# Attention results divided two heads per position at a time, and ScalarE zeroing the first key blocks

## The reference

```
x = x + tanh(g_xattn[0]) * retention(ln(x), ctx)                  # 2 heads of 128, group norm, gate
x = x + tanh(g_ffn[0])   * mixture_of_experts(ln(x))              # 8 experts, the first of the top 2
x = x + tanh(g_xattn[1]) * grouped_attention(ln(x), ctx)          # 32 query heads, 8 key/value groups, head size 8
x = x + tanh(g_ffn[1])   * sparse_ffn(ln(x))                      # 256 -> 1024, 2:4 sparsified, -> 256

# grouped_attention, as far as the change touches it
attn = softmax(masked_scores)                     # causal, per head
out  = einsum('bnghm,bmgd->bnghd', attn, v)       # here: unnormalized sums, and a ninth column with the sum of weights
return out.reshape(B, S, D) @ w_o.T + b_o
```

## Time and profile before

| | us |
|---|---|
| median of 3 runs | 356.65 (356.33 to 358.82) |
| the profiled execution | 355.62 |
| its span | 353.5 |
| TensorE busy in the span | 316.3 (89%) |
| VectorE busy | 265.9 (75%) |
| ScalarE busy | 167.6 (47%) |
| GpSimd busy | 109.6 (31%) |

### The profile page before, as it was taken

The page is one execution under the profiler, slowest core; times in us unless marked ns, Lnnn a source line. Parts: engine busy times, 40 slices in busy tenths (PEclk is TensorE's granted clock), DMA queues, the critical chain, the costliest instruction groups (busy, mean ns, idle before and its releaser), DMA issues.

```text
span 353.5 us, 5149 instructions
## 1 busy us (share of the span) xinstructions
PE 316.3 (89%) x1671; PEld 218.0 (62%) x1671; DVE 265.9 (75%) x582; ACT 167.6 (47%) x341; POOL 109.6 (31%) x156
## 2 busy tenths in 40 slices
PE   2899886669999988999989999998979999899997
PEld 1495675647899634554644564463443787688896
DVE  4348896675677749989967996897585559999992
ACT  2433464344444223136767765775685434333320
POOL 7502675172000275601333424433555101000000
PEclk9999999559999999999999999999999999999999
DMA  6999300025321213700000000000000000000001
GB/s 231 359 413 295 67 1 16 2 89 174 106 67 59 77 59 111 307 0 9 0 7 2 0 1 9 0 3 0 7 2 1 0 2 0 2 0 1 30 32 59
DMA packets 14090, 22.96 MB, mean 65 GB/s; under 512 B 2065, under 2 KB 11409, under 8 KB 13202
## 3 DMA queue, kind: packets, MB, share of 16 engines
q1 hardware_dynamic: 13298, 20.56, 17.2%
q0 software_dynamic: 768, 2.10, 1.8%
HBM read 16.36 MB, written 6.03 MB: 63 GB/s over the span
## 4 chain that ended last, share of the span: by engine, by line
PE 57%; DVE 20%; issue 7%; POOL 6%; DMA 5%; ACT 4%; SPq 1%; DVEq 0%; ACTq 0%; POOLq 0%
PE bank L276 40%; DVE mx L1351 7%; PE bank L496 5%; PE bank L464 4%; ACT region L1024 3%; DVE stats L1097 3%; PE bank L467 2%; POOL x_sorted L821 2%; PE bank L292 2%; POOL rstd L789 2%; DVE x_sb L1137 1%; PE bank L511 1%; PE bank L286 1%; DMA x_sb<-in_x_dram 1%; DVE kblk L1270 1%
## 5 line engine op out<-in xcount | busy, mean ns | idle before, releaser
L1024 ACT ACTIVATE region<-bank,padcol 128x512 f32<-128x512 f32 x96 | 62.3, 692 | 18.7 <-PE bank L276 17.9
L1351 DVE TENSOR_REDUCE mx<-bank 128x2 f32<-128x512 f32 (+1 forms) x96 | 60.9, 683 | 4.8 <-PE bank L467 4.4
L857 POOL TENSOR_SCALAR_AFFINE_SELECT region<-region 128x1024 f32<-128x1024 f32 x32 | 35.8, 1121 | 77.9 <-ACT region L1024 77.8
L276 PE MATMUL bank<-qst,kblk 128*128 128x512 f32 x96 | 45.7, 487 | 0.8 <-DMA qst<-nmT 0.3
L464 PE MATMUL bank<-kblk,qst 128*128 128x512 f32 x96 | 43.6, 470 | 1.6 <-DVE mx L1351 1.2
L467 PE MATMUL bank<-causb,identb 128*128 128x256 bf16 (+1 forms) x96 | 30.6, 319 | 0.0
L789 POOL TENSOR_TENSOR rstd<-veps,power 128x1 f32<-128x1 f32 x40 | 25.7, 643 | 3.3
L785 POOL TENSOR_SCALAR veps<-mv 128x1 f32<-128x1 f32 x40 | 12.8, 320 | 40.7 <-DVE mv L1099 40.6
L276 PEld LDWEIGHTS bank<-qst,kblk 128*128 128x128 f32 x96 | 18.5, 197 | 9.2 <-ACT region L1024 6.6
L496 PE MATMUL bank<-region,vaug 128*32 128x512 f32 x192 | 23.9, 600 | 0.2
L464 PEld LDWEIGHTS bank<-kblk,qst 128*128 128x128 f32 x96 | 18.3, 190 | 8.8 <-issue 4.1
(11 more groups left out here) (205 smaller groups left out, 783.7 us busy)
## 6 DMA issues: line engine op xcount, KB each, us to landing
e_gu<-in_e_gu_dram SPq DMA_DIRECT2D x2, 1408.0 KB, 12.3
x_sorted<-zero SPq DMA_DIRECT2D x1, 1920.0 KB, 9.6
y_sorted<-region SPq DMA_DIRECT2D x15, 128.0 KB, 1.7
x_sb<-in_x_dram SPq DMA_DIRECT2D x4, 256.0 KB, 4.0
ctxT<-in_ctxT_dram SPq DMA_DIRECT2D x2, 512.0 KB, 6.4
e_down<-in_e_down_dram SPq DMA_DIRECT2D x1, 1024.0 KB, 14.0
region<-x_sorted SPq DMA_DIRECT2D x1, 1024.0 KB, 7.6
e_gu<-in_f_gate_dram SPq DMA_DIRECT2D x1, 1024.0 KB, 6.2
```

The lines of the kernel that those rows point to most:

```text
L276: return pe.matmul(dst, lhsT, rhs, start=first, stop=last)
L857: pool.affine_select(out=block, in_=block, compare_op=ALU.is_ge, fill=0.0, base=0, pattern=[[0, 2], [0, PER_GROUP], [1, P]], channel_multi ...
L1024: taken(act.activation(dst, src.rearrange("p (h n) -> p h n", n=SEQ - mt * P), ACT.Exp, bias=padcol[:, key:key + 1], scale=float(HD) ** -0 ...
L1351: taken(dve.reduce_max(mx[:, b % 2, nt, quads, q, hg], src, AX), "sa")
```

## The change

Two things. The division in `finish` is done for two head positions at a time: c = 0 and c = 2 now each make four transposes into the whole of bank 6, one reciprocal of 128x16 and one product of 128x128; c = 1 and c = 3 do nothing. Counts of semaphores follow. And `kblk[0]` is zeroed by ScalarE, with two copies of 128x1024 from the tile of zeros, behind the last copy to `xT` and ahead of the routing's exponential; GpSimd's two memsets and its wait for them are gone. `kblk[1]` is still zeroed by GpSimd.

```
+HEAD_PAIRS = (0, 2)
-        rden = sb("rden", [P, 2, HALVES, QUADS])
+        rden = sb("rden", [P, 2, 2, GROUPS])
 # TensorE, finish
-                if c < PER_GROUP:
-                    f = 4 * i + c
+                if c in HEAD_PAIRS:
+                    f = 2 * i + c // 2
                     dst = acquire(pe, "avT", f, "turn1")
 ...
-                    for q in range(HALVES):
-                        ins = pe.transpose(dst[:, tile_cols(q)], avT[nt][:, q, c * P:(c + 1) * P], ident[:, :])
+                    for h in range(2):
+                        for q in range(HALVES):
+                            ins = pe.transpose(dst[:, tile_cols(HALVES * h + q)], avT[nt][:, q, tile_cols(c + h)], ident[:, :])
                     ready(ins, "avT")
                 elif c == PER_GROUP:
-                    pe.wait_ge(sem("avT_taken"), 4 * i + 4)
+                    pe.wait_ge(sem("avT_taken"), 2 * i + 2)
                     turn_pair("atT", i, att[:, i % 2, :], "turn1")
-                else:
+                elif c > PER_GROUP:
 # GpSimd
-            pool.wait_ge(sem("res0_ready"), TILES)
-            pool.wait_ge(sem("rs_taken"), RET_HEADS)
-            clear_blocks(0)
-            pool.wait_ge(sem("blocks_clear"), HALVES)
-
 # ScalarE
+            act.wait_ge(sem("constants_set"), 1)
+            act.wait_ge(sem("res0_ready"), TILES)
+            act.wait_ge(sem("rs_taken"), RET_HEADS)
+            for q in range(HALVES):
+                act.activation(kblk[0][q], zero[:, :].unsqueeze(1).to_broadcast([P, QUADS, SEQ]), ACT.Copy)\
+                   .then_inc(sem("blocks_clear"), 1)
+
             act.wait_ge(sem("routed"), 2)
             act.activation(r_s[:, 3, :], r_s[:, 2, :], ACT.Exp).then_inc(sem("tanh_vexp"), 1)
 ...
-                        act.wait_ge(sem("avT_ready"), 8 * (b - 1) + 4 * nt + 4)
+                        act.wait_ge(sem("avT_ready"), 4 * (b - 1) + 2 * nt + 2)
 # VectorE, finish (value_copy has the same new count)
-                if c < PER_GROUP:
-                    o = att[:, i % 2, :].rearrange("p (q j h d) -> p h q j d", q=HALVES, j=QUADS, h=PER_GROUP)
-                    f = 4 * i + c
-                    src = filled(dve, "avT", f)[:, 0:2 * P].rearrange("p (q j r) -> p q j r", q=HALVES, j=QUADS)
+                if c in HEAD_PAIRS:
+                    o = att[:, i % 2, :].rearrange("p (g h d) -> p h g d", g=GROUPS, h=PER_GROUP)
+                    f = 2 * i + c // 2
+                    src = filled(dve, "avT", f).rearrange("p (h g r) -> p h g r", h=2, g=GROUPS)
                     dve.reciprocal(rden[:, f % 2, :, :], src[:, :, :, HD]).then_inc(sem("rden_made"), 1)
                     dve.wait_ge(sem("rden_made"), f + 1)
-                    taken(dve.tensor_tensor(out=o[:, c, :, :, :], in0=src[:, :, :, 0:HD],
-                                            in1=rden[:, f % 2, :, :].unsqueeze(3).to_broadcast([P, HALVES, QUADS, HD]),
+                    taken(dve.tensor_tensor(out=o[:, c:c + 2, :, :], in0=src[:, :, :, 0:HD],
+                                            in1=rden[:, f % 2, :, :].unsqueeze(3).to_broadcast([P, 2, GROUPS, HD]),
                                             op=ALU.mult), "avT")
```

More of the change, by code:

```diff
@@ L1388, in value_copy @@
                 if b >= 1:
-                    dve.wait_ge(sem("avT_ready"), 8 * (b - 1) + 4 * nt + 4)
+                    dve.wait_ge(sem("avT_ready"), 4 * (b - 1) + 2 * nt + 2)
                 taken(dve.tensor_copy(avT[nt][:, 0, :], src), "av0")
```

## The result

| | before | after |
|---|---|---|
| median, same chip | 356.49 us (355.0 to 358.82, 4 runs) | 352.08 us (350.91 to 352.6, 4 runs) |
| ratio | | 0.9887, interval 0.9856 to 0.9919 |
| profiled execution | 355.62 | 352.60 |
| its span | 353.5 | 350.8 |

The change makes the kernel 1.1% faster, 4.41 us by the medians, against 4.82 predicted. By the interval the gain of the runs lies between 2.9 and 5.1 us. The lines of the program have moved: L1197 is now L1201, L1402 is L1406, L1404 is L1408, L511 is L513 and L276 is L277.

What follows compares the result with a forecast made beforehand. It took routing's cross-engine chain, and VectorE pacing TensorE in passes 1 and 2, as the bounds. Clear 1.52 plus pairs 3.30 made 4.82 us, so 356.65 - 4.82 = 351.8 us (chance 0.45), range 349.6 to 355.4.

Steps and rivals of the forecast that it cites:

- Line 1197 (1.52 us): Routing: without GpSimd's memsets beside it, VectorE's second instruction falls from 1.90 to 0.38 us, gaining 1.52.
- So what is gained at line 1197 goes through scatter and load to the slots: Routing to expert slots: the first slot turn waits for the scattered tiles' load, so the 1.52 us arrives there.
- ScalarE's copies cost nothing: Routing: two clears, 2.09 us in all, fit in ScalarE's idle time before the exponential, with 1.2 us to spare.
- First tiles (0.82 us): Passes 1 and 2, first tile: TensorE's stalls behind VectorE go, 0.41 us each, 0.82 together.
- Second tiles (2.48 us): Passes 1 and 2, second tile: TensorE's stalls and waits at the `att` turn go, 0.75 and 1.73 us.
- The feared wait at the turn of the negated maxima in pass 2: Pass 2: TensorE comes up to 2.1 us earlier, VectorE only about 0.2, so a wait can come back; part of rival 1.
- A pair's cost (0.45 us): VectorE's division: one paired reciprocal and product take 0.45 us, ends 0.44 and 0.74; a tile falls from 1.48 to 0.90.
- Pass 3 and the last block (0): Pass 3 and last block: pairs gain 0, since ScalarE paces the one and TensorE has no gap in the other.
- Rival 1: Attention passes: VectorE's next piece holds TensorE instead, a third of the 3.30 us stays, time 354.0 us; chance 0.25.
- Rival 2: Routing: with less idle time the logits run at 2.4 GHz, 0.86 us less, time 350.9 us; chance 0.14.
- Rival 3: Passes 1 and 2: VectorE idles 0.27 us at each of eight fills awaiting four transposes, time 357.3 us; chance 0.08.
- Rival 4: Routing: line 1197 is long for another reason or ScalarE's copies hold it up, time 353.3 us; chance 0.08.

Runs made afterwards that it cites:

- the change again: The same changed program timed once more against the kernel before, beside its halves: 351.65 us, ratio 0.9889.
- clear only: The changed kernel with the division put back to four turns, keeping ScalarE's clear: 354.98 us, ratio 0.9975 against before.
- pairs only: The changed kernel with the clear given back to GpSimd, keeping the division by pairs: 352.99 us, ratio 0.9922 against before.
- batches 0 and 1: The changed kernel with pairs only in passes 1 and 2; batches 2 and 3 keep four turns: 351.86 us, ratio 0.9870 against before.
- GpSimd later: The changed kernel with GpSimd's memsets instead of ScalarE's copies, behind VectorE's second instruction of line 1197: 351.23 us, ratio 0.9869 against before.
- three warm matmuls: Pairs and GpSimd's clear after line 1197, with four of seven keep-warm matmuls ahead of the first slot turn left out: 352.10 us, ratio 0.9881 against before.

## Why the prediction was right, and where it was not

The time, 352.08, lies 0.3 us above the 351.8 predicted, with the mechanism forecast as the likeliest. The interval of the gain, 2.9 to 5.1 us, is far wider than that, so the closeness of 0.3 is in part luck. Of its two terms the pairs were right for their reasons; the clear was right at its source, and part of it was lost on the way.

- **Line 1197 (1.52 us): right.** 1.90 to 0.41, 1.49. In before the memsets take 949 to 952 ns each, beside line 1197 and elsewhere alike, so GpSimd loses nothing and VectorE alone is held until 0.14 us after the second memset's end. The row of before:
```profile
L810 POOL MEMSET kblk<- x4: 949/951/952, 60.4 to 122.6; 128x1024 f32 x4
```
The Trainium skill (SBUF — State Buffer, SBUF: two separate sides) says that an instruction of VectorE in a mode that uses two ports and one of GpSimd contend for a shared pair of SBUF ports, an exclusive lock: whichever starts first gets it for the whole instruction, and the other blocks. The traces agree in substance: the memset that started 0.08 us earlier kept its 951 ns, and with the memsets behind VectorE's instruction both run at full speed. In which mode line 1197 ran no trace shows. Only the end does not fit a lock held without a break over both memsets, for then VectorE would have ended 0.38 us behind them and not 0.14.
- **"So what is gained at line 1197 goes through scatter and load to the slots": half wrong.** This step did not hold. Of 1.47 us at the place, TensorE's own chain took 0.41 at the slots in the trace of after (and 0.5 in the change again, none in clear only), and the landing of the last store another 0.83. By the medians the clear is worth 0.83 (before less clear only) to 1.34 us (pairs only less the change), where 1.52 was forecast; the runs alone do not exclude 1.52 (0.83 may be 0.0 to 1.7), the losses are read from the traces. The sum looked at the slots alone and did not follow the gain to the next DMA on the path.
- **ScalarE's copies cost nothing: right where it was costed** (1.99 us for 2.09, 1.37 idle left), but the longer landing was seen in just the traces that have them. The prediction had no term for anything 60 us later. What held the store up was a packet of instructions (last section).
- **First tiles (0.82 us): right.** 6.28 became 5.89 in pass 1, 0.39 for 0.41. The window of 6.00 us shows TensorE busy throughout: it paces now.
- **Second tiles (2.48 us): right to 0.2.** The turn of the negated maxima in pass 1 moved from 216.32 to 215.28, which is 1.08 by pass 1's own start, against 0.41 + 0.75 = 1.16. Pass 2 gave the rest, including the whole 0.94 at `att`. What is missing is the new wait of 0.20 on a maximum at 237.20. The feared wait at the turn of the negated maxima in pass 2 did not grow: TensorE idles 0.42 us there before and after.
- **A pair's cost (0.45 us): low by 0.04.** The page after, by line: 128x16 reciprocals took 251 ns where 128x8 took 199, products the 292 of the earlier trace rows.
```profile
L1408 DVE TENSOR_TENSOR att<-bank,rden 128x128 f32<-128x128 f32 x16 | 4.7, 292 | 0.5
L1406 DVE RECIPROCAL rden<-bank 128x16 f32<-128x16 f32 x16 | 4.0, 251 | 4.9 <-PE bank L513 4.9
```
- **Pass 3 and the last block (0): right**, by the kernel with pairs for two batches (0.13 us).
- **Rival 1, stalls come back:** one of 0.20 us, not a third of 3.30. Although VectorE is 99% busy in the first-tile window, the maxima keep up there.
- **Rival 2, the clock stays up:** not in the trace of after (1.72 us for the logits), but in four of the seven other traces with a short line 1197. It brought the place a further 7.73 - 7.05 = 0.68 us forward, against 0.86 priced. The four with fast logits gained 0.83 to 2.14 us up to pass 1, on average 1.47, the four with slow ones 0.30 on average. The same program shows both (after and the change again), so this was a matter of the single execution, not a case that holds or fails for a kernel.
- **Rival 3, starved fills:** no. Four transposes were done by 192.45 + 0.60 = 193.05, 0.36 us ahead of the reciprocal, and none of the eight reciprocals of passes 1 and 2 waits for its fill.
- **Rival 4, the clear pays nothing:** no at the source; over the whole kernel it pays 0.83 of 1.52 us by the medians.

## What to carry to other kernels

Where an engine's instruction is several times as long as its twin, look for one on GpSimd or VectorE that runs beside it, and move the cheaper of the two past the other: a wait of one instruction was worth as much as a change of engine. Follow a gain through every DMA on the path and ask at each join which side came last and by how much; here 0.4 us at one and a longer landing at another took about half of it by the medians. When a transfer lands late, look for the packets of other queues that lie among its own. Fewer hand-overs of a single bank, and less work for its reader, paid only in the stages whose windows show that reader full.

## What the hardware showed

- **A store that lands late behind a block of instructions.** The last `y_sorted` store took 2.17 to 2.63 us in the five traces with ScalarE's copies of zeros 57 us earlier, and 1.68 to 1.83 in the five others. The packet records show what stands in between. The page counts ten packets on queue 14 that carry the program's own instructions:
```profile
q14 instruction: 10, 0.08, 0.1%
```
  One of 8 KB falls on this store in every trace. In the five late ones it starts among the store's packets, and the last eight of those, 1 KB each, start within 0.01 us of its end. In after it runs from 122.30 to 123.06, the eight start at 123.05, and all others had started by 122.62. In the five short ones it starts behind the store's last 1 KB packet (before: 123.40 behind 123.38). In four of the late traces it takes 0.54 to 0.76 us, and the landing is 0.49 to 0.82 us longer; in the fifth (batches 0 and 1) it takes 0.31 and the landing is 0.95 longer, so there something else adds. In those four it starts 0.96 to 0.97 us behind the store's issue, in the short ones 1.30 to 1.31. Whose instructions it carries, and whether the two copies added to ScalarE's program bring it forward, no run shows.
- **The first two indirect DMAs trade places.** With GpSimd's memsets ahead of the scatter (before, pairs only, both with GpSimd later) the first starts 1.04 to 1.05 us behind the place and the second takes 1.57; without them it is 0.47 to 0.48 and 2.17. The sum is the same, 11.03 us to the eighth in before and 11.07 after, so nothing comes of it. The cause was not sought.
- **The clock's return varies.** The granted clock was back at 2.4 GHz between 77.64 (clear only) and 81.86 us (pairs only). Counted from the place this was at 11.3 to 12.9 us in the four traces with all seven warm matmuls in which the slots opened at 17.08 to 17.24, and at 14.2 to 14.4 in the five in which TensorE's own chain opened them at 17.61 to 17.74; with three warm matmuls it was 14.2 and the load came last all the same. The gain of the clear up to pass 1 lay between 1.98 and -0.95 us over the five traces with ScalarE's clear.
